# Starting two steps of the next attention block ahead of the last token tile's transposes

## The chip, the cores and the metric

The kernel runs on all 8 cores of one Trainium2 chip. Each core computes one batch element of the input, on its own, with no exchange between cores. The metric is the device time of one execution in microseconds (us), that of the slowest core.

Engines are named as the profile names them: PE is TensorE (PEld its weight loads), DVE is VectorE, ACT is ScalarE, POOL is GpSimd, SP is SyncE. A "q" behind an engine's name is its sequencer.

## The reference

```python
x = L0_attn_x                                  # 8 x 4096 x 1024, float32
q, k, v = x @ w_q, x @ w_k, x @ w_v            # one head of 128
A = softmax(q @ k.T / sqrt(128))               # 4096 x 4096 for each batch element
x = layernorm(x + ((A @ v) * mask) @ w_o)
# feed-forward with ternary weights and activations rounded to 8 bits a row
gate = silu(act_quant(x) @ quant(w_gate).T)    # 1024 -> 4096
up   = act_quant(x) @ quant(w_up).T
x = layernorm(x + act_quant(gate * up) @ quant(w_down).T)
```

`quant(w)` needs the mean of |w| over the whole matrix, then turns each weight into -1, 0 or 1 times a scale. `act_quant` needs the largest |x| of each row.

## The kernel before

The program is written engine by engine: each of three phases has one block per engine, and the order within a block is the order of the code. Engines meet only at semaphores (`sm[...]`), which count up.

**Phase AB** (`_phase_AB`) is the one that is changed. First q, k and v are projected (`qt`, `kt`, `vt`), and v is transposed to `vtok`. Then the attention runs over 8 blocks `qb` (0 to 7) of 512 queries. A block has a *loop* and a *tail*.

- The loop runs over 32 steps `kc` of 128 keys. In a step PE multiplies the scores into `ps_s` (L566), ACT takes the exponential of them into `pbuf` (L478), and PE adds `pbuf` times v into `ps_h` (L570) and the row sums into `ps_r` (L572). `ps_s` and `pbuf` have two buffers each, and PE's waits let the scores of step kc+1 be computed only behind the products of step kc (L566 to L574).
- The tail takes 4 tiles of 128 tokens (`sc` = 4·qb to 4·qb+3). When the loop's last sum is there (`avrs`), DVE copies the sums to `rsb` and takes their reciprocal. For each tile PE multiplies by w_o into `ps_y1` (L598, L600), DVE adds the residual, makes the layer norm (with a square root on ACT in its middle, L496), and rounds the row to `xqdq` (L438, semaphore `xqd`). PE then transposes `xqdq` into `ps_tr` with 8 small products (`_xtr`, L590, semaphore `xtr`), and ACT copies `ps_tr` to `xqs` (`_xtre`, L490, semaphore `xtre`). `ps_tr` has one buffer, so each set of transposes waits for the copy of the one before.

The copies lag. ACT copies the tiles 4·qb and 4·qb+1 in the tail, and the last two tiles at the head of the next block (L471 to L473, `_xtre_head`). PE transposes the tile 4·qb+2 in the tail, behind the products of the last tile, and the last tile 4·qb+3 at the head of the next block (L552 to L559), ahead of everything else there.

DVE has a second job in this phase, the weights. Ahead of the loops' end in blocks 0, 1 and 2 it sums |w| over 32 chunks of 128 x 1024 each (`w1_chunks`, L349), which SP loads from HBM into the two buffers `wstf`. From block 4 on it turns the chunks into ternary weights, 6 behind each tile (`w2_chunks`, L442), and POOL stores them. Between blocks 2, 3 and 4 PE has a tiny product at the block's head (L543, L548), which makes the weight scales.

**Phase C1** computes gate and up (L783, L789) with the ternary weights, and rounds and transposes the result. **Phase C2** multiplies by w_down (L946) and makes the second layer norm.

Of the kernel before, what the change touches and what calls it, by code (L numbers as in the profile page):

```python
# [22 lines left out]
NHC = D // P  # L23
# [110 lines left out]
def _phase_AB(nc, sm, d, pers):  # L134
    ones_b = pers["ones_b"]; onesf = pers["onesf"]; ones1f = pers["ones1f"]
    identb = pers["identb"]; identf = pers["identf"]
# [7 lines left out]
             (d["wuT"], d["wuqs"], NHC, 4, 1024, 1),  # L144
             (d["wdT"], d["wdqs"], NOC, 1, 1024, 2)]
    n_wch = sum(r * c for _, _, r, c, _, _ in wplan)
    wsched = []
    for c in range(4):
# [13 lines left out]
    def SB(name, shape, dt):  # L162
        return es.enter_context(nc.sbuf_tensor(name, shape, dt))
    def PS(name, shape, dt):
        return es.enter_context(nc.psum_tensor(name, shape, dt))
    with es:
# [20 lines left out]
        xqdq = SB("xqdq", [P, 2, D], BF16)  # L187
# [6 lines left out]
        ps_tr = PS("ps_tr", [P, 1024], BF16)  # L194
# [250 lines left out]
        @blk.scalar  # L445
        def _(s):
            s = _AD(s)
            def _xtre_head(s, sc):
                j = sc % 4
                s.wait_ge(sm["xtr"], sc + 1)  # L450
                if sc >= 4 and j == 0:
                    qbp = sc // 4 - 1
                    s.wait_ge(sm["xqsp0" if qbp % 2 == 0 else "xqsp1"],
                              16 * NHC * (qbp // 2 + 1))
                s.copy(xqs[:, :, j * 128:(j + 1) * 128],
                       ps_tr[:].rearrange("p (a b) -> p a b", a=8)
                       ).then_inc(sm["xtre"], 1)
            for sb in range(NQB):
                s.wait_ge(sm["qkv"], (sb + 1) * 3)
                s.copy(qt[:, sb * 512:(sb + 1) * 512], ps_s[:, 0, :])  # L460
                s.copy(kt[:, sb * 512:(sb + 1) * 512], ps_s[:, 1, :])
                s.copy(vt[:, sb * 512:(sb + 1) * 512], ps_h[:]
                       ).then_inc(sm["qkve"], 1)
            for gidx in range(8):
                s.wait_ge(sm["vtr"], gidx + 1)
                s.copy(vtok[:, gidx * 4:(gidx + 1) * 4, :],
                       ps_vt[:].rearrange("p (a b) -> p a b", a=4)
                       ).then_inc(sm["vtre"], 1)
            for qb in range(NQB):
                base = qb * 32  # L470
                if qb >= 1:  # L471
                    for scp in (qb * 4 - 2, qb * 4 - 1):
                        _xtre_head(s, scp)  # L473
                for kc in range(32):
                    s.wait_ge(sm["ss"], base + kc + 1)
                    if kc >= 2:
                        s.wait_ge(sm["avrs"], base + kc - 1)
                    s.activation(pbuf[:, kc % 2, :], ps_s[:, kc % 2, :],  # L478
                                 ACTF.Exp, bias=0.0, scale=ATT_SCALE
                                 ).then_inc(sm["pexp"], 1)  # L480
                s.wait_ge(sm["avrs"], (qb + 1) * 32)
                s.copy(htb[:], ps_h[:]).then_inc(sm["hev"], 1)
                def _xtre(s, sc):
                    j = sc % 4
                    s.wait_ge(sm["xtr"], sc + 1)
                    if sc >= 4 and j == 0:
                        qbp = sc // 4 - 1
                        s.wait_ge(sm["xqsp0" if qbp % 2 == 0 else "xqsp1"],
                                  16 * NHC * (qbp // 2 + 1))
                    s.copy(xqs[:, :, j * 128:(j + 1) * 128],  # L490
                           ps_tr[:].rearrange("p (a b) -> p a b", a=8)
                           ).then_inc(sm["xtre"], 1)
                for j in range(4):
                    sc = qb * 4 + j
                    s.wait_ge(sm["z1"], 2 * (sc + 1))
                    s.activation(stats[:, 5:6], stats[:, 4:5], ACTF.Sqrt,  # L496
                                 bias=0.0, scale=1.0).then_inc(sm["sqrt1"], 1)
                    if j >= 2:
                        _xtre(s, sc - 2)
                if qb == NQB - 1:  # L500
                    _xtre(s, qb * 4 + 2)
                    _xtre(s, qb * 4 + 3)

        @blk.tensor
        def _(t):
# [32 lines left out]
            for qb in range(NQB):  # L538
                base = qb * 32
                qsl = slice(qb * 512, (qb + 1) * 512)  # L540
                if qb == 3:
                    t.wait_ge(sm["wabs"], n_wch + 1)
                    t.matmul(pv32[0:1, 0:4], onesf[:], wacc[:],  # L543
                             start=True, stop=True)
                    t.drain().then_inc(sm["wsum"], 1)
                if qb == 4:
                    t.wait_ge(sm["wscal"], 1)
                    t.matmul(pv32[:, 4:12], ones1f[:], srow[:],  # L548
                             start=True, stop=True)
                    t.drain().then_inc(sm["wbc"], 1)  # L550
                if qb >= 1:
                    sc3 = qb * 4 - 1  # L552
                    t.wait_ge(sm["xqd"], sc3 + 1)
                    t.wait_ge(sm["xtre"], sc3)
                    for ic in range(NHC):
                        t.transpose(ps_tr[:, ic * 128:(ic + 1) * 128],
                                    xqdq[:, sc3 % 2, ic * 128:(ic + 1) * 128],
                                    identb[:])
                    t.drain().then_inc(sm["xtr"], 1)  # L559
                    t.wait_ge(sm["hev"], qb)  # L560
                    t.wait_ge(sm["rdone"], qb)
                    t.wait_ge(sm["pexp"], base)
                for kc in range(32):
                    if kc >= 2:
                        t.wait_ge(sm["pexp"], base + kc - 1)
                    t.matmul(ps_s[:, kc % 2, :], kt[:, kc * 128:(kc + 1) * 128],  # L566
                             qt[:, qsl], start=True, stop=True
                             ).then_inc(sm["ss"], 1)
                    t.wait_ge(sm["pexp"], base + kc + 1)
                    t.matmul(ps_h[:], vtok[:, kc, :], pbuf[:, kc % 2, :],  # L570
                             start=(kc == 0), stop=(kc == 31))
                    t.matmul(ps_r[:], ones_r[:], pbuf[:, kc % 2, :],  # L572
                             start=(kc == 0), stop=(kc == 31)
                             ).then_inc(sm["avrs"], 1)  # L574
                t.wait_ge(sm["rdone"], qb + 1)
                if qb >= 1:
                    t.wait_ge(sm["z1"], 8 * qb)
                for j in range(4):
                    t.transpose(ps_y1[:, 0, j:j + 1],
                                rinv[0:1, j * 128:(j + 1) * 128],  # L580
                                identf[0:1, 0:1])
                t.drain().then_inc(sm["rcolT"], 1)
                t.wait_ge(sm["hev"], qb + 1)
                t.wait_ge(sm["rcole"], qb + 1)
                def _xtr(t, sc):
                    t.wait_ge(sm["xqd"], sc + 1)
                    if sc >= 1:
                        t.wait_ge(sm["xtre"], sc)
                    for ic in range(NHC):
                        t.transpose(ps_tr[:, ic * 128:(ic + 1) * 128],  # L590
                                    xqdq[:, sc % 2, ic * 128:(ic + 1) * 128],
                                    identb[:])
                    t.drain().then_inc(sm["xtr"], 1)
                for j in range(4):
                    sc = qb * 4 + j
                    if sc >= 1:
                        t.wait_ge(sm["z1"], 2 * sc)
                    t.matmul(ps_y1[:, 0, :], htb[:, j * 128:(j + 1) * 128],  # L598
                             wob[:, 0:512], start=True, stop=True)
                    t.matmul(ps_y1[:, 1, :], htb[:, j * 128:(j + 1) * 128],  # L600
                             wob[:, 512:1024], start=True, stop=True
                             ).then_inc(sm["y1"], 1)
                    if j >= 1:
                        _xtr(t, qb * 4 + j - 1)
                if qb == NQB - 1:
                    _xtr(t, qb * 4 + 3)
# [371 lines left out]
```

## Time and profile before

| | us |
|---|---|
| median of 2 runs | 4078.61 (4067.52 and 4089.70) |
| the profiled execution, its own time | 4072.59 |
| its span on the slowest core (core 5) | 4070.8 |
| spans of the 8 cores | 4046.7 to 4070.8 |
| granted TensorE clock, mean of each core | 0.695 to 0.697 |
| busy on core 5: PE / DVE / ACT | 2086.7 / 2291.9 / 535.4 |

All positions below are microseconds from the start of the span of core 5. The attention's loops and tails run from 160 to about 1745, C1 from there to about 3500, C2 to the end. A row of the timeline gives the start, the duration, the engine, the line, the operation with output and input, and in brackets how long the engine had been idle before it and what ended that. L53 and L54 are the lines of a helper, which issues most instructions of DVE, ACT and POOL; there the names of the tiles tell which one it is. `ps_y` in a row is `ps_y1` here.

### The profile page before, as it was taken

The numbers are of one execution on the slowest core, as the hardware profiler recorded it, in microseconds if no ns is written. First come the engines' busy times: TensorE is split into PE (matmuls) and PEld (weight loads), VectorE is DVE, ScalarE is ACT, GpSimd is POOL, SyncE is SP. The second block draws the span as 40 slices with busy tenths as digits, with TensorE's granted clock in tenths as the row PEclk, the third lists the DMA queues.
The fourth block names the chain that finished last, engine by engine and source line by source line (L and its number), as shares of the span: only waits on it lengthen the run. The fifth ranks groups of instructions, "written<-read, shape, count | busy, mean of one in ns | idle before, by whom it ended". The sixth has DMA issues, their size and how long they took to land. (4 is left out here: it accounts for less than half of the span.)

```text
span 4070.8 us, 32582 instructions; the slowest of 8 cores (4046.7 to 4070.8 us)
## 1 busy us (share of the span) xinstructions
PE 2086.7 (51%) x8516; PEld 937.5 (23%) x8516; DVE 2291.9 (56%) x3888; ACT 535.4 (13%) x794; POOL 244.0 (6%) x359
## 2 busy tenths in 40 slices
PE   4535244250413214047483929384756657179998
PEld 2312111120101101012231313132322223124443
DVE  2145653517365463736757575857576666535555
ACT  0212111120201111001211111111111111100000
POOL 1000000001101010100000000000000000000000
PEclk8655555555555555579695959697877879589999
DMA  8405241105344251444242424333333332364441
GB/s 238 134 31 175 93 134 42 36 26 140 97 114 124 67 147 60 134 140 135 63 143 54 146 62 128 87 116 94 104 104 93 114 83 83 84 209 138 159 135 62
DMA packets 290771, 440.43 MB, mean 108 GB/s; under 512 B 12960, under 2 KB 220832, under 8 KB 290592
## 3 DMA queue, kind: packets, MB, share of 16 engines
q1 hardware_dynamic: 240784, 285.77, 24.4%
q0 software_dynamic: 49808, 152.59, 12.4%
q8 instruction: 74, 1.21, 0.1%
q14 instruction: 105, 0.86, 0.1%
HBM read 337.64 MB, written 100.66 MB: 108 GB/s over the span
## 5 line engine op out<-in xcount | busy, mean ns | idle before, releaser
L783 PE MATMUL ps_g<-wgu,xqr 128*128 128x512 bf16 x2048 | 496.4, 386 | 151.8 <-issue 92.4
L946 PE MATMUL ps_y<-wdq,hqr 128*128 128x512 bf16 x2048 | 453.9, 382 | 69.5 <-DMA wdq<-wdqs 59.1
L789 PE MATMUL ps_u<-wgu,xqr 128*128 128x512 bf16 x2048 | 485.2, 380 | 0.0
L803 PE MATMUL ps_t<-identb,hq 128*128 128x128 bf16 x1024 | 129.5, 307 | 581.8 <-DVEq L743 455.6
L53 DVE TENSOR_SCALAR gtr<-ps_g,scv 128x512 f32<-128x512 f32 x256 | 192.1, 750 | 250.1 <-PEq L794 249.9
L570 PE MATMUL ps_h<-pbuf,vtok 128*128 128x512 f32 x256 | 195.9, 765 | 244.6 <-ACTq L54 244.6
L53 DVE TENSOR_TENSOR hp<-sgt,ps_u 128x512 f32<-128x512 f32 x256 | 175.8, 687 | 241.8 <-ACTq L54 241.8
L590 PE MATMUL ps_tr<-identb,xqdq 128*128 128x128 bf16 x200 | 25.3, 307 | 526.2 <-ACTq L54 435.1
L783 PEld LDWEIGHTS ps_g<-wgu,xqr 128*128 128x128 bf16 x2048 | 184.4, 98 | 458.8 <-issue 282.3
L53 ACT ACTIVATE sgt<-gtr 128x512 f32<-128x512 f32 x256 | 161.1, 629 | 874.0 <-DVEq L54 874.0
L946 PEld LDWEIGHTS ps_y<-wdq,hqr 128*128 128x128 bf16 x2048 | 199.2, 98 | 323.9 <-issue 93.5
L789 PEld LDWEIGHTS ps_u<-wgu,xqr 128*128 128x128 bf16 x2048 | 201.3, 98 | 245.1 <-issue 6.3
L803 PEld LDWEIGHTS ps_t<-identb,hq 128*128 128x128 bf16 x1024 | 99.1, 138 | 614.0 <-issue 614.0
L53 DVE COPY rsb<-ps_r 1x512 f32<-1x512 f32 x8 | 5.4, 679 | 417.2 <-PE ps_r L572 416.8
L53 ACT ACTIVATE pbuf<-ps_s 128x512 fp32r<-128x512 f32 x256 | 152.9, 597 | 482.6 <-PE ps_s L566 482.5
L53 DVE TENSOR_REDUCE stats<-wstf 128x1 f32<-128x1024 f32 x96 | 117.1, 1220 | 172.6 <-DMA wstf<-wgT 66.8
L53 ACT COPY hqts<-ps_t 128x1024 bf16<-128x1024 bf16 x128 | 129.6, 1012 | 576.7 <-PEq L807 576.7
L53 DVE TENSOR_SCALAR wc<-wstf,whm 128x1024 f32<-128x1024 f32 x192 | 144.7, 754 | 80.8 <-DMA wstf<-wgT 25.5
L53 DVE TENSOR_REDUCE stats<-hp 128x1 f32<-128x512 f32 x256 | 175.6, 686 | 21.5 <-issue 1.3
L53 DVE SCALAR_TENSOR_TENSOR z2t<-ps_y,yscale,x1r 128x512 f32<-128x512 f32 x64 | 48.0, 751 | 223.7 <-PEq L951 221.3
L570 PEld LDWEIGHTS ps_h<-pbuf,vtok 128*128 128x128 f32 x256 | 73.5, 287 | 419.9 <-issue 419.9
L677 POOL DMA_DIRECT2D hqTs<-hqts x32 | 63.6, 1987 | 1715.2 <-ACTq L54 1715.2
(104 smaller groups left out, 2371.9 us busy)
## 6 DMA issues: line engine op xcount, KB each, us to landing
wgu<-wgqs SPq DMA_DIRECT2D x64, 1024.0 KB, 7.5
wgu<-wuqs SPq DMA_DIRECT2D x64, 1024.0 KB, 9.8
wstf<-wgT SPq DMA_DIRECT2D x64, 512.0 KB, 4.9
wstf<-wuT SPq DMA_DIRECT2D x64, 512.0 KB, 4.8
wstf<-wdT SPq DMA_DIRECT2D x64, 512.0 KB, 3.9
hqTs<-hqts POOLq DMA_DIRECT2D x32, 1024.0 KB, 8.5
hqr<-hqTs SPq DMA_DIRECT2D x32, 1024.0 KB, 9.9
xts<-xT POOLq DMA_DIRECT2D x8, 2048.0 KB, 14.3
```

Of the source, the lines that this page charges most:

```text
L53: f(*a, **k)
L570: t.matmul(ps_h[:], vtok[:, kc, :], pbuf[:, kc % 2, :], start=(kc == 0), stop=(kc == 31))
L590: t.transpose(ps_tr[:, ic * 128:(ic + 1) * 128], xqdq[:, sc % 2, ic * 128:(ic + 1) * 128], identb[:])
L677: gp.dma_start(out=d["hqTs"].rearrange("(a p) s -> p a s", p=P)[:, :, gsc * 128:(gsc + 1) * 128], in_=hqts[:, gsc % 2, :, :]).then_inc(sm[ ...
L783: t.matmul(ps_g[:, sc % 2, :], xqr[:, sb % 2, ic, sc * 128:(sc + 1) * 128], wgu[:, idx % 2, 0, ic, :], start=(ic == 0), stop=(ic == NHC - 1))
L789: t.matmul(ps_u[:, sc % 2, :], xqr[:, sb % 2, ic, sc * 128:(sc + 1) * 128], wgu[:, idx % 2, 1, ic, :], start=(ic == 0), stop=(ic == NHC - 1))
L803: t.transpose(ps_t2[:, k * 128:(k + 1) * 128], hq[:, gsc % 2, oc * 128:(oc + 1) * 128], identb[:])
L946: t.matmul(ps_y2[:, sc % 3, hf, :], hqr[:, pr % 4, oc, (sc % 2) * DH:(sc % 2 + 1) * DH], wdq[:, oc, hf * 512:(hf + 1) * 512], start=(oc == ...
```

## The change

Three pieces of code move; nothing is computed otherwise. On ACT the two copies at a block's head (tiles 4·qb-2 and 4·qb-1) move behind the exponential of the block's step 1. On PE the transposes of tile 4·qb-1 move from ahead of the block's step 0 into its step 1, between the scores and the wait for the exponential. The waits of the block's head for `hev`, `rdone` and `pexp` stay ahead of step 0.

```diff
@@ ACT
             for qb in range(NQB):
                 base = qb * 32
-                if qb >= 1:
-                    for scp in (qb * 4 - 2, qb * 4 - 1):
-                        _xtre_head(s, scp)
                 for kc in range(32):
                     s.wait_ge(sm["ss"], base + kc + 1)
                     if kc >= 2:
...
                                  ACTF.Exp, bias=0.0, scale=ATT_SCALE
                                  ).then_inc(sm["pexp"], 1)
+                    if qb >= 1 and kc == 1:
+                        _xtre_head(s, qb * 4 - 2)
+                        _xtre_head(s, qb * 4 - 1)
@@ PE
                 if qb >= 1:
-                    sc3 = qb * 4 - 1
-                    t.wait_ge(sm["xqd"], sc3 + 1)
-                    t.wait_ge(sm["xtre"], sc3)
-                    for ic in range(NHC):
-                        t.transpose(ps_tr[:, ic * 128:(ic + 1) * 128],
-                                    xqdq[:, sc3 % 2, ic * 128:(ic + 1) * 128],
-                                    identb[:])
-                    t.drain().then_inc(sm["xtr"], 1)
                     t.wait_ge(sm["hev"], qb)
                     t.wait_ge(sm["rdone"], qb)
                     t.wait_ge(sm["pexp"], base)
...
                     t.matmul(ps_s[:, kc % 2, :], kt[:, kc * 128:(kc + 1) * 128],
                              qt[:, qsl], start=True, stop=True
                              ).then_inc(sm["ss"], 1)
+                    if qb >= 1 and kc == 1:
+                        sc3 = qb * 4 - 1
+                        t.wait_ge(sm["xqd"], sc3 + 1)
+                        t.wait_ge(sm["xtre"], sc3)
+                        for ic in range(NHC):
+                            t.transpose(ps_tr[:, ic * 128:(ic + 1) * 128],
+                                        xqdq[:, sc3 % 2,
+                                             ic * 128:(ic + 1) * 128],
+                                        identb[:])
+                        t.drain().then_inc(sm["xtr"], 1)
                     t.wait_ge(sm["pexp"], base + kc + 1)
                     t.matmul(ps_h[:], vtok[:, kc, :], pbuf[:, kc % 2, :],
```

PE, from the end of block 0's tail into block 1, in the kernel before:

```order
L598 MATMUL ps_y<-wob,htb 128x512
L600 MATMUL ps_y<-wob,htb 128x512
L590 MATMUL ps_tr<-identb,xqdq 128x128 x8
L556 MATMUL ps_tr<-identb,xqdq 128x128 x8
L566 MATMUL ps_s<-qt,kt 128x512
L570 MATMUL ps_h<-pbuf,vtok 128x512
L572 MATMUL ps_r<-pbuf,ones_r 1x512
L566 MATMUL ps_s<-qt,kt 128x512
L570 MATMUL ps_h<-pbuf,vtok 128x512
```

The same place in the changed kernel, whose lines have other numbers (its L558 is L566 before, its L566 is L556 before, its L572 and L574 are L570 and L572):

```order
L600 MATMUL ps_y<-wob,htb 128x512
L602 MATMUL ps_y<-wob,htb 128x512
L592 MATMUL ps_tr<-identb,xqdq 128x128 x8
L558 MATMUL ps_s<-qt,kt 128x512
L572 MATMUL ps_h<-pbuf,vtok 128x512
L574 MATMUL ps_r<-pbuf,ones_r 1x512
L558 MATMUL ps_s<-qt,kt 128x512
L566 MATMUL ps_tr<-identb,xqdq 128x128 x8
L572 MATMUL ps_h<-pbuf,vtok 128x512
L574 MATMUL ps_r<-pbuf,ones_r 1x512
```

The 8 transposes of the last tile moved behind 4 products of the next block: the scores, the product with v and the sums of step 0, and the scores of step 1. This holds in blocks 1 to 7.

ACT at the same place, the changed kernel against the one before (`stats` is the square root, `xqs` the copies, `pbuf` the exponentials):

```order
 L53 COPY xqs<-ps_tr 128x8x128
 L53 ACTIVATE stats<-stats 128x1
-L53 COPY xqs<-ps_tr 128x8x128 x3
-L53 ACTIVATE pbuf<-ps_s 128x512 x32
+L53 COPY xqs<-ps_tr 128x8x128
+L53 ACTIVATE pbuf<-ps_s 128x512 x2
+L53 COPY xqs<-ps_tr 128x8x128 x2
+L53 ACTIVATE pbuf<-ps_s 128x512 x30
```

Of the three copies in a row the first stays behind the last square root of the tail, and the other two moved behind the second exponential.

## Rows read from the trace of the kernel before

**Rows 1.** Windows: a tail, a loop, most of phase C1; busy us by engine, PE clock.
```profile
242.00:319.00 77.00, 9.37 (x44) 5.60 (x44) 60.92 (x120) 5.53 (x9) 3.71 (x7) 0.50 0.14 48
...
654.00:737.00 83.00, 51.95 (x96) 19.69 (x96) 0.20 (x1) 21.12 (x35) 4.81 (x9) 0.50 0.06 19
...
1745.00:2900.00 1155.00, 690.46 (x3291) 312.00 (x3292) 742.84 (x1178) 186.09 (x246) 41.14 (x23) 0.79 0.37 103
```

**Rows 2.** Who waited for whom, 150 to 1745: us in total, times, longest.
```profile
DVE rsb L53 <- PE ps_r L572: 416.8, 6, 88.0
...
PE ps_tr L556 <- DVEq L54: 54.6, 7, 8.2
```

**Rows 3.** Timeline of the first head, between block 0's tail and block 1's loop.
```profile
308.70 1.01 PE L590 MATMUL ps_tr<-identb,xqdq 128*128 128x128 bf16 x8 [14.50 <-ACTq L54]
...
316.39 1.22 DVE L53 SCALAR_TENSOR_TENSOR xqdq<-tiq,c1q 128x1024 bf16<-128x1024 int32 x1
...
317.89 1.01 PE L556 MATMUL ps_tr<-identb,xqdq 128*128 128x128 bf16 x8 [8.18 <-DVEq L54]
319.02 1.01 ACT L53 COPY xqs<-ps_tr 128x1024 bf16<-128x1024 bf16 x1 [8.18 <-PEq L559]
...
319.35 0.77 PE L566 MATMUL ps_s<-qt,kt 128*128 128x512 f32 x1 [0.44 <-issue]
...
320.19 1.28 ACT L53 ACT_TABLE_LOAD   x1 [0.16 <-PE ps_s L566]
...
321.49 0.60 ACT L53 ACTIVATE pbuf<-ps_s 128x512 fp32r<-128x512 f32 x1
...
322.25 0.77 PE L570 MATMUL ps_h<-pbuf,vtok 128*128 128x512 f32 x1 [2.14 <-ACTq L54]
...
323.97 0.60 ACT L53 ACTIVATE pbuf<-ps_s 128x512 fp32r<-128x512 f32 x1 [1.88 <-PE ps_s L566]
...
324.73 0.77 PE L570 MATMUL ps_h<-pbuf,vtok 128*128 128x512 f32 x1 [0.86 <-ACTq L54]
```

**Rows 4.** Timeline of PE and DVE: the ends of the loops of blocks 1, 2, 3.
```profile
401.59 0.63 PE L572 MATMUL ps_r<-pbuf,ones_r 128*1 128x512 f32 x1
...
409.81 0.68 DVE L53 COPY rsb<-ps_r 1x512 f32<-1x512 f32 x1 [0.19 <-issue]
...
570.11 0.63 PE L572 MATMUL ps_r<-pbuf,ones_r 128*1 128x512 f32 x1
...
575.76 0.68 DVE L53 COPY rsb<-ps_r 1x512 f32<-1x512 f32 x1 [0.23 <-issue]
...
736.79 0.68 DVE L53 COPY rsb<-ps_r 1x512 f32<-1x512 f32 x1 [83.67 <-PE ps_r L572]
```

**Rows 5.** Timeline of PE: the heads of blocks 3, 4 and 6.
```profile
652.38 1.01 PE L556 MATMUL ps_tr<-identb,xqdq 128*128 128x128 bf16 x8 [7.41 <-DVEq L54]
...
806.07 0.56 PE L548 MATMUL ps_vt<-srow,ones1f 1*128 1x8 f32 x2 [0.23 <-issue]
...
813.66 1.01 PE L556 MATMUL ps_tr<-identb,xqdq 128*128 128x128 bf16 x8 [7.04 <-DVEq L54]
...
1274.19 1.01 PE L556 MATMUL ps_tr<-identb,xqdq 128*128 128x128 bf16 x8 [7.83 <-DVEq L54]
```

**Rows 6.** Groups of DVE by line, 150 to 1745: count, busy us, mean ns.
```profile
L53 DVE TENSOR_REDUCE stats<-wstf 128x1 f32<-128x1024 f32 x66 | 80.5, 1220 | 90.2 <-DMA wstf<-wdT 41.4 <-DMA wstf<-wuT 25.3 <-DMA wstf<-wgT 22.4
...
L53 DVE TENSOR_REDUCE stats<-z1t 128x1 f32<-128x1024 f32 x32 | 39.0, 1220 | 3.8
```

**Rows 7.** Timeline of PE at the start of phase C1.
```profile
1782.02 3.57 PE L783 MATMUL ps_g<-wgu,xqr 128*128 128x512 bf16 x8 [54.01 <-DMA wgu<-wuqs]
...
1785.38 2.83 PE L789 MATMUL ps_u<-wgu,xqr 128*128 128x512 bf16 x8
...
1793.11 1.89 PE L783 MATMUL ps_g<-wgu,xqr 128*128 128x512 bf16 x8 [1.19 <-DVEq L54]
...
1794.83 1.89 PE L789 MATMUL ps_u<-wgu,xqr 128*128 128x512 bf16 x8
```

## The prediction

> **What bounds the kernel now.** I read the windows first, to see which engine each stretch hangs on. A tail (242 to 319) has DVE busy for 60.92 of its 77 us and PE for 9.37; a loop (654 to 737) has PE busy for 51.95 of 83 and DVE for 0.20 [rows 1]. So loops and tails stand one behind the other, each on its own chain, and what one leaves unused of the other's engine is lost. Then the waits: DVE waits for a loop's last sum 6 times in 8, 416.8 us in all, and PE waits for the rounded last tile at all 7 heads, 54.6 us in all, 7.8 each [rows 2]. That second wait is what the change goes at.
>
> The timeline of the first head shows it from inside [rows 3]. PE is free at 308.70 + 1.01 = 309.71, with the transposes of tile 2 done. DVE still rounds tile 3, until 316.39 + 1.22 = 317.61. PE's transposes of tile 3 start at 317.89, and only behind them come the scores of step 0 (319.35), a table load on ACT (320.19, 1.28), the exponential (321.49) and the product with v (322.25). The product of step 1 starts at 324.73. The loop's steps 0 and 1 need nothing of tile 3.
>
> Last the loops' ends, which tell in which blocks an earlier PE is worth anything [rows 4]. In block 3 the copy to `rsb` was released by PE, after 83.67 us of idle DVE. In blocks 1 and 2 it was not: PE's last sum ended at 402.22 and 570.74, and DVE came at 409.81 and 575.76, straight from its own weight chunks (idle 0.19 and 0.23). There DVE is late by 7.6 and 5.0 us. The 6 waits of rows 2 are blocks 0 and 3 to 7.
>
> **The change part by part.** No instruction is added or removed; the order moves at 7 heads.
>
> *PE, the new head.* Set on the clock of rows 3: the scores of step 0 start 0.44 behind PE's last instruction, as they do now, at 310.15. The first product with v comes 2.90 later (322.25 - 319.35, with the table load in it), at 313.05; it, the sums and the scores of step 1 follow. The second exponential starts 1.72 behind that product (323.97 - 322.25) and takes 0.60: 315.37. Then ACT copies tile 2: 0.16 to start, as behind `ps_s`, and 1.01, to 316.54, and PE knows it 0.28 later (317.61 to 317.89 is the same step from DVE). So the chain that the change puts ahead of the transposes is 0.44 + 2.90 + 1.72 + 0.60 + 0.16 + 1.01 + 0.28 = 7.11 us long, and it lies in a gap of 8.18. The transposes still start at 317.89, on the wait for DVE. Behind them the product of step 1 starts as the scores of step 0 did, 1.46 later (319.35 - 317.89), its exponential long there: at 319.35 instead of 324.73. **A head gains 5.38 us.**
>
> *ACT.* The copy of tile 3 stands ahead of the exponential of step 2. It ends at 319.02 + 1.01 = 320.03, as now; the exponential of step 2 can't start before 319.35 + 1.72 = 321.07. So the copy delays nothing, and `xqs` is complete, and stored by POOL, at the time it is now.
>
> *How thin the cover is.* The gap that must hold the 7.11 us is 7.41 in block 3, 7.04 in block 4 (behind the small product of L548, which ends at 806.63), 7.83 in block 6 [rows 5]; of 54.6 us in 7, none of the others is under 7.8. Block 4 loses 0.07; the rest lose nothing.
>
> *What the table load costs.* The row has 1.28 us, and the exponential starts 0.02 behind it [rows 3]. That is the price I use, and it now lies beside DVE's work. The Trainium skill (page ScalarE: Activation LUTs, section What ACT_TABLE_LOAD costs) counts a drain of about 1.38 us on top, 2.66 for a switch. This case's trace shows no such drain between the load and the exponential. By the page the chain would be over 8.4 us and longer than every gap, and the gain smaller by up to 4.4 us.
>
> *Copies between exponentials.* They could ask for further table loads. In the rows now a copy stands ahead of the load and `Exp` behind it; no row has an `xqs` copy under `Exp`. I take nothing; the bound above is one load (1.28) in front of the copies and one in front of step 2, below.
>
> *Which heads count.* Heads 3 to 7 pass on what they gain: 5 x 5.38 - 0.07 = 26.8 us. In blocks 1 and 2 PE gains 5.38 too and then waits longer for DVE, whose chunks come no earlier (they start behind tile 3 and wait for SP's loads). **0 there.** Below: 0 at all heads, if a wait that I don't see takes over; above: all 7, 37.7 us, if the chunks happened to come faster.
>
> *What runs beside.* For 7 us a head PE and ACT now work next to DVE's layer norm. A DVE reduction of 128 x 1024 takes 1220 ns in the tail (of `z1t`, PE nearly idle) and 1220 ns over the weight chunks, most of which run beside a loop [rows 6]. So I charge nothing. The clock can't fall: it is at 0.50 (1.2 GHz) in loop and tail alike [rows 1].
>
> *The sum.* The profiled execution took 4072.6 us; less 26.8 that is 4045.8. It lies 6.0 below the median of the two runs (4078.6), from which the sum gives 4051.8. I take the middle, **4049**. C1 and C2 come earlier by 27 us and are otherwise the same.
>
> **The rivals.**
>
> *A. All seven heads count.* DVE's slack in blocks 1 and 2 would have to be gone. Against it stand idle times of 0.19 and 0.23 on DVE there. Gain 37.7: 4038.
>
> *B. Nothing is gained.* The wait for tile 3 only moves by two steps, and something later in the block takes the 5 us back. For it: the wait is still there. Against it: each step of a loop waits only for the step before. 4076.
>
> *C. More table work on ACT.* A copy that changes the table would put 1.28 ahead of tile 2's copy: the chain is 8.39, past the gaps of blocks 3 and 4 by 0.98 and 1.35, of the three others by up to 0.56 each. With another load ahead of step 2 (ready at 321.3, not 321.1) it is some 5 us in all: 4054. The page's rule above, with its 1.38, would end at the same 4053 to 4054.
>
> *D. Slower: phase C1 meets a lower clock.* C1 starts 27 us earlier against whatever sets its clock, which averages 0.79 there [rows 1]. At 1.2 GHz 8 gate products start within 3.36 us (1782.02 to 1785.38), at 2.4 GHz within 1.72 (1793.11 to 1794.83) [rows 7]; a group of 16 costs 3.3 us more at the lower level. If over 8 more of C1's 256 groups fall there, and PE is what those wait for, the gain is gone; with 12 more it is 4049 + 40 = 4089. For it: the two runs before lie 22 us apart. Against it: nothing in C1 depends on when it starts.
>
> **How the numbers follow.** The forecast has 0.80, A 0.05, B 0.05, C 0.06, D 0.04. All of them but a far end of A or D lie within 2% (82 us) of before, which is about what a measurement can tell from no change: faster by more 0.01, within 0.98, slower by more 0.01. The scatter of the runs is 11 us to either side of their median. The range takes that around 4049, with A and C inside: 4034 to 4070; it leaves out B and D.
>
> **What would show it right or wrong.** In the profile after: at each head PE's scores of step 0 directly behind the transposes of tile 2; the transposes of tile 3 released by DVE and not by ACT, after some 3 us of idle and not 8; the product of step 1 some 1.5 us behind their start. PE's wait for the rounded tile shrinks from 7.8 to about 3 a head. The `rsb` copies of blocks 1 and 2 stay where they are, and from block 3 on each comes 5.4 us earlier than the last, C1's first product 27 us earlier than 1782. The count of table loads stays. Wrong would be: `rsb` of block 1 or 2 released by DVE later than now, the tile-3 transposes released by ACT, or C1 at another clock.

## The result and the profile after

The changed kernel takes 4041.4 us (median of 12 runs, 4032.7 to 4061.1) against 4067.5 for the kernel before (11 runs). The ratio is 0.9934, 95% interval 0.9917 to 0.9952: 27 us less, between 20 and 34. In some executions the cores of one die are granted a lower clock and take longer; the ratios leave these executions out. The profiled execution took 4037.0 us; its slowest core is core 6, with a span of 4035.1.

The timeline of the first head in the kernel after answers to [rows 3]. Its lines are two higher than before; L558 is the scores, L566 the transposes of tile 3, L572 the product with v.

```profile
307.41 1.01 PE L592 MATMUL ps_tr<-identb,xqdq 128*128 128x128 bf16 x8 [14.50 <-ACTq L54]
...
308.86 0.77 PE L558 MATMUL ps_s<-qt,kt 128*128 128x512 f32 x1 [0.44 <-issue]
309.71 1.28 ACT L53 ACT_TABLE_LOAD   x1 [2.47 <-PE ps_s L558]
311.00 0.60 ACT L53 ACTIVATE pbuf<-ps_s 128x512 fp32r<-128x512 f32 x1
...
311.76 0.77 PE L572 MATMUL ps_h<-pbuf,vtok 128*128 128x512 f32 x1 [2.14 <-ACTq L54]
...
313.48 0.60 ACT L53 ACTIVATE pbuf<-ps_s 128x512 fp32r<-128x512 f32 x1 [1.88 <-PE ps_s L558]
314.23 1.01 ACT L53 COPY xqs<-ps_tr 128x1024 bf16<-128x1024 bf16 x1 [0.15 <-issue]
...
316.63 1.01 PE L566 MATMUL ps_tr<-identb,xqdq 128*128 128x128 bf16 x8 [3.25 <-DVEq L54]
317.75 1.01 ACT L53 COPY xqs<-ps_tr 128x1024 bf16<-128x1024 bf16 x1 [2.51 <-PEq L570]
317.87 0.76 PE L572 MATMUL ps_h<-pbuf,vtok 128*128 128x512 f32 x1 [0.23 <-issue]
```

The scores of step 0 start 0.44 behind the transposes of tile 2, the table load now runs while DVE still works on tile 3, and the transposes of tile 3 are still released by DVE, after 3.25 us of idle and not 8.18. The product of step 1 starts 1.24 behind their start; before it was 324.73 - 317.89 = 6.84. This head gains 5.60 us.

The ends of the loops of blocks 1 to 4 on DVE, and the heads of blocks 4 and 6, in the timeline of the kernel after:

```profile
411.46 0.68 DVE L53 COPY rsb<-ps_r 1x512 f32<-1x512 f32 x1 [0.18 <-issue]
...
574.16 0.68 DVE L53 COPY rsb<-ps_r 1x512 f32<-1x512 f32 x1 [0.23 <-issue]
...
729.67 0.68 DVE L53 COPY rsb<-ps_r 1x512 f32<-1x512 f32 x1 [78.06 <-PE ps_r L574]
...
799.99 0.77 PE L558 MATMUL ps_s<-qt,kt 128*128 128x512 f32 x1 [0.44 <-issue]
...
805.07 1.22 DVE L53 SCALAR_TENSOR_TENSOR xqdq<-tiq,c1q 128x1024 bf16<-128x1024 int32 x1
805.36 1.01 ACT L53 COPY xqs<-ps_tr 128x1024 bf16<-128x1024 bf16 x1 [0.15 <-issue]
...
806.58 1.01 PE L566 MATMUL ps_tr<-identb,xqdq 128*128 128x128 bf16 x8 [2.07 <-ACTq L54]
...
885.40 0.68 DVE L53 COPY rsb<-ps_r 1x512 f32<-1x512 f32 x1 [78.20 <-PE ps_r L574]
...
1252.29 1.01 PE L566 MATMUL ps_tr<-identb,xqdq 128*128 128x128 bf16 x8 [2.87 <-DVEq L54]
```

Blocks 1 and 2 still end on DVE, with 0.18 and 0.23 of idle [rows 4]; block 3's wait is 78.06 in place of 83.67. In block 4, the one with no cover to spare, ACT's copy ends at 806.37 and DVE's rounding at 806.29, and the transposes are released by ACT. The distance between the `rsb` copies of blocks 2 and 4 holds two heads, two loops and two tails without weight chunks, and so is free of what DMA adds elsewhere: 898.08 - 575.76 = 322.3 us before, 885.40 - 574.16 = 311.2 after, 5.5 a head. Below it is "distance 2 to 4".

The profile has the same copies on the other cores. Over the 8 cores of each profiled execution, the mean distance from block 2's to block 7's copy, which holds the five heads 3 to 7, fell from 1007.0 to 978.7 us: 28.3, or 5.7 a head. The mean distance from block 0's to block 2's, which holds heads 1 and 2, was 335.9 before (330.0 to 340.8 on single cores) and 334.8 after (333.1 to 337.5): no gain that stands out of that spread. And a tail is as long as before: from block 1's copy to the transposes of its last tile, next to which PE and ACT now work, it is 76.62 us before (409.81 to 486.43) and 76.63 after (411.46 to 488.09).

Who waited for whom, 150 to 1755, kernel after:

```profile
DVE rsb L53 <- PE ps_r L574: 390.0, 6, 91.4
...
PE ps_tr L566 <- DVEq L54: 17.8, 6, 3.2
```

PE's wait for the rounded tile fell from 54.6 us in 7 [rows 2] to 17.8 in 6, and the seventh is a wait of 2.1 for ACT. Windows of 1750 us of phase C1, before (1755 to 3505) and after (1720 to 3470):

```profile
1755.00:3505.00 1750.00, 1061.94 (x5064) 479.37 (x5064) 1140.90 (x1809) 284.46 (x378) 60.14 (x31) 0.80 0.35 100
```

```profile
1720.00:3470.00 1750.00, 1054.01 (x4976) 479.55 (x5064) 1141.95 (x1810) 284.79 (x378) 60.50 (x31) 0.80 0.33 100
```

The mean clock is 0.80 in both; C1 only starts earlier (1782.02 before, 1746.35 after). These 35.7 us are more than the measured 27, as they compare two single executions on different cores.

### The profile page after: what moved, and what is told of

It reads as the page before. It is cut to its first block and busy times, and to the rows that moved or that the text cites. A ratio compares the mean times of both kernels' runs of the same rounds, so it can differ in the third digit from the quotient of the medians.

```text
span 4035.1 us, 32453 instructions; the slowest of 8 cores (4013.1 to 4035.1 us)
## 1 busy us (share of the span) xinstructions
PE 2075.0 (51%) x8387; PEld 936.5 (23%) x8516; DVE 2293.0 (57%) x3888; ACT 535.4 (13%) x794; POOL 245.0 (6%) x359
## 5 line engine op out<-in xcount | busy, mean ns | idle before, releaser
L572 PE MATMUL ps_h<-pbuf,vtok 128*128 128x512 f32 x256 | 195.9, 765 | 240.4 <-ACTq L54 238.6
L592 PE MATMUL ps_tr<-identb,xqdq 128*128 128x128 bf16 x200 | 25.3, 306 | 524.1 <-ACTq L54 432.9
L572 PEld LDWEIGHTS ps_h<-pbuf,vtok 128*128 128x128 f32 x256 | 73.5, 287 | 412.5 <-issue 412.5
```

The costliest lines, as they stand in the source:

```text
L572: t.matmul(ps_h[:], vtok[:, kc, :], pbuf[:, kc % 2, :], start=(kc == 0), stop=(kc == 31))
L592: t.transpose(ps_tr[:, ic * 128:(ic + 1) * 128], xqdq[:, sc % 2, ic * 128:(ic + 1) * 128], identb[:])
```

## The experiments

Ratios are to the kernel before in the same series, whose median was 4062 to 4065 us; the microseconds beside them are the ratio times that. Single positions are those of the slowest core. Which heads count comes first, then how far the steps can be moved, then what bounds the loop.

**Only heads 1 and 2, only heads 3 to 7**

```diff
-                    if qb >= 1 and kc == 1:
+                    if 1 <= qb <= 2 and kc == 1:
```

with the code of before at the other heads; the second kernel has `qb >= 3` there.

> The new order at heads 1 and 2 alone; heads 3 to 7 as before. Theory (those heads are absorbed by DVE's weight chunks): PE's last sum of blocks 1 and 2 ends 5 to 6 us earlier against the head, DVE copies to rsb when it did before, with under 0.3 us of idle, and the time stays within the scatter, about 0 us of gain. Rival (every head counts alike): 2 x 5.6 = 11 us less than before, and rsb released by PE.

Ratio 1.000 (0.998 to 1.002). The timeline of this kernel, PE's last sum of block 2 and DVE behind it:

```profile
578.27 0.63 PE L586 MATMUL ps_r<-pbuf,ones_r 128*1 128x512 f32 x1
...
587.36 0.68 DVE L53 COPY rsb<-ps_r 1x512 f32<-1x512 f32 x1 [0.23 <-issue]
```

PE ends 587.36 - 578.90 = 8.5 us ahead of DVE, where it was 5.0 before, and DVE takes no notice. How much of the 3.5 is the head can't be read, since the chunks themselves come a few us earlier or later in each execution. But DVE's copies come no sooner: block 0's to block 2's is 336.8 us on the mean of the 8 cores, against 335.9 before. The rival's 11 us lie outside the interval, which reaches to 8 us of gain.

> The new order at heads 3 to 7 alone. Theory: 5 x 5.6 = 28 us less than before, as much as the whole change. Rival (every head counts alike): 5/7 of the change's 26 us, 19 us.

Ratio 0.9937 (0.9924 to 0.9951): 26 us (20 to 31), the whole change; the rival's 19 lie just outside. Distance 2 to 4 is 311.1.

**The first pass's chunks split 48, 24, 24**

```diff
-                    w1_chunks(32)
+                    w1_chunks((48, 24, 24)[qb])
```

> The kernel before, with the 96 weight chunks of the first pass split 48, 24, 24 over blocks 0, 1, 2 in place of 32, 32, 32. Theory (DVE ends the loops of blocks 1 and 2, 7.6 and 5.0 us behind PE): rsb of blocks 1 and 2 is released by PE, 12.6 us less than before. Rival (PE sets these ends too): 0.

> The changed kernel with the same 48, 24, 24. Theory: now all 7 heads count, so it lies 7 x 5.6 = 39 us below the kernel before with that split, 52 us below the kernel before. Rival (heads 1 and 2 give nothing for another reason than DVE's chunks): 28 us below that kernel, 41 below the kernel before.

The ratios are 0.9971 (0.9953 to 0.9989), 12 us, and 0.9868 (0.9849 to 0.9886), 54 us (46 to 61); the rivals' 0 and 41 lie outside. The `rsb` copies of blocks 1 and 2 in the timeline, the order of before first, the changed one second:

```profile
398.37 0.68 DVE L53 COPY rsb<-ps_r 1x512 f32<-1x512 f32 x1 [15.27 <-PE ps_r L572]
...
559.42 0.68 DVE L53 COPY rsb<-ps_r 1x512 f32<-1x512 f32 x1 [19.91 <-PE ps_r L572]
```

```profile
401.54 0.68 DVE L53 COPY rsb<-ps_r 1x512 f32<-1x512 f32 x1 [9.88 <-PE ps_r L574]
...
557.16 0.68 DVE L53 COPY rsb<-ps_r 1x512 f32<-1x512 f32 x1 [14.89 <-PE ps_r L574]
```

Now PE releases both. From one to the other it is 161.05 us with the old order (165.95 in [rows 4]), and 155.62 with the new: 4.9 us were DVE's lateness, and a further 5.4 are the head, which was worth nothing as long as DVE came last. Block 1 shows the same. From block 0's copy to its own it is 167.99 us in the kernel before (from 241.82 to 409.81), 160.56 with the other split (from 237.81) and 155.00 with the new order as well (from 246.54): 7.4 and 5.6.

**One step in place of two**

```diff
-                    if qb >= 1 and kc == 1:
+                    if qb >= 1 and kc == 0:
```

> The transposes and both copies move by one step (into step 0) in place of two. Theory: what counts is the work put ahead of DVE's rounded tile: the first product with v comes 1.24 us behind the start of the transposes in place of 4.36, 3.1 us a head (the table load among them), 16 us in all. Rival (the gain comes from the hidden table load and not from the steps): the same 28 us as with two steps. Rival (the load stays on the path): 1.8 us a head, 9 us.

Distance 2 to 4 is 899.63 - 583.61 = 316.0, that is 3.15 a head, as expected. In the first head:

```profile
316.01 1.01 PE L566 MATMUL ps_tr<-identb,xqdq 128*128 128x128 bf16 x8 [6.97 <-DVEq L54]
317.25 0.76 PE L572 MATMUL ps_h<-pbuf,vtok 128*128 128x512 f32 x1 [0.23 <-issue]
```

The ratio, 0.9983 (0.9963 to 1.0003), is 7 us, between 15 and nothing, where 16 were expected. The heads show no loss: from block 2's to block 7's copy it is 990.0 us on the mean of the 8 cores, 17.0 less than before, so the five heads give what was expected. A part of the shortfall stands ahead of them: block 0's to block 2's copy, where DVE's chunks decide, took 339.7 us (333.2 to 345.3 on single cores) against 335.9 before. Whether the order of this kernel delays these chunks or the execution had them late isn't shown, and the rest is open.

**Two steps, but the copy of tile 2 left at the head**

```diff
+                if qb >= 1:
+                    _xtre_head(s, qb * 4 - 2)
                 for kc in range(32):
...
-                        _xtre_head(s, qb * 4 - 2)
```

> As the change, but ACT's copy of tile 2 stays at the head, ahead of the exponential of step 0. Theory (the cover hides ACT's chain whole, but for 0.07 us in block 4): the same time as the change, 28 us below before, and the transposes of all 7 heads released by DVE, block 4's too. Rival (the copy's place matters, as it delays the first exponential or the table load): 1 us a head, 5 us slower than the change. The distance of the rsb copies of blocks 2 and 4: 311.2 by the theory, over 312 by the rival.

Ratio 0.9937 (0.9913 to 0.9961), distance 311.2. In the waits all 7 transposes are released by DVE:

```profile
PE ps_tr L567 <- DVEq L54: 19.9, 7, 3.2
```

So ACT's two copies are hidden whole. The time alone couldn't tell (16 to 35 us less than before, which holds the rival's 23); the distance does.

**Three steps**

```diff
-                    if qb >= 1 and kc == 1:
+                    if qb >= 1 and kc == 2:
```

> As the change, but both copies and the transposes one step later still, in step 2. Theory (the cover is 8.18 us and the chain ahead of the transposes, 7.11 us in the change, is now 2.53 longer, 9.64): the transposes are released by ACT and no more by DVE, PE stands still for the copy of tile 2, and a head gains 6.7 us against before, 1.1 more than the change and not 2.5 more; some 33 us in all. Rival (the wait for DVE's rounded tile still decides): 8.1 us a head, 40 us. Judged by the distance of the rsb copies of blocks 2 and 4, which holds two heads and no weight chunks: 322.3 us before, 311.2 with the change; 309.0 by the theory, 306.2 by the rival.

Ratio 0.9922 (0.9904 to 0.9939), 32 us. The waits turn over:

```profile
PE ps_tr L566 <- ACTq L54: 14.6, 7, 2.1
```

Distance 2 to 4 is 310.8, not 309.0. The theory was right and its sum careless: it took the gap of the first head, 8.18, for heads 3 and 4, whose gaps are 7.41 and 7.04 [rows 5], 0.77 and 1.14 less. With those the gain is 5.9 and 5.6 in place of 6.7, and 322.3 - 11.5 = 310.8. Past the cover PE stands still for ACT's copy. The time alone doesn't part this kernel from the change (25 to 39 us against 20 to 34), but the rival's 40 lie just outside.

**Step 4, with the copy of tile 2 still in step 1**

```diff
                     if qb >= 1 and kc == 1:
                         _xtre_head(s, qb * 4 - 2)
+                    if qb >= 1 and kc == 4:
                         _xtre_head(s, qb * 4 - 1)
...
-                    if qb >= 1 and kc == 1:
+                    if qb >= 1 and kc == 4:
                         sc3 = qb * 4 - 1
```

> The copy of tile 2 behind the exponential of step 1 as in the change, but the transposes of tile 3 in step 4 and its copy behind the exponential of step 4. Theory (the loop may start whenever PE is free, and the transposes then fit into PE's idle time of a step): the first product with v comes 9.2 us earlier than before, the transposes cost 0.3 us behind the 0.92 us that PE idles in a step: 8.9 us a head, 44 us in all. Rival (transposes and copy in a running loop cost their full 2.4 us): 6.8 us a head, 34 us. Rival (the wait for tile 3 was all there was to gain, and the change has it): no more than the change, 28 us.

Ratio 0.9895 (0.9880 to 0.9910): 43 us (37 to 49), 16 more than the change, outside both rivals. The head as it stands in PE's timeline:

```profile
316.53 0.77 PE L573 MATMUL ps_h<-pbuf,vtok 128*128 128x512 f32 x1 [0.92 <-ACTq L54]
...
317.52 0.63 PE L559 MATMUL ps_s<-qt,kt 128*128 128x512 f32 x1
317.95 1.08 PE L567 MATMUL ps_tr<-identb,xqdq 128*128 128x128 bf16 x8
...
319.26 0.77 PE L573 MATMUL ps_h<-pbuf,vtok 128*128 128x512 f32 x1 [0.23 <-issue]
```

The transposes wait for nobody. The product comes 319.26 - 316.53 = 2.73 us behind the one of step 3, against 2.53 in an ordinary step: they cost 0.20. Distance 2 to 4 is 304.8 on the slowest core and 305.7 on the mean of the 8.

**The orders side by side**

Means over the 8 cores of each profiled execution, in us between `rsb` copies. The last column is the gain of the five heads 3 to 7 against before, and behind it the gain that was expected for them, as far as a sum was on record.

| order | block 0 to 2 | 2 to 4 | 2 to 7 | gain of five heads |
|---|---|---|---|---|
| before | 335.9 | 322.4 | 1007.0 | |
| new at heads 1 and 2 | 336.8 | 322.4 | 1005.9 | 1.1 (0) |
| one step | 339.7 | 316.1 | 990.0 | 17.0 (16) |
| two steps, the change | 334.8 | 311.2 | 978.7 | 28.3 (26.8) |
| two steps at heads 3 to 7 | 337.3 | 311.2 | 977.3 | 29.6 (28) |
| two steps, a copy left | 334.5 | 311.2 | 977.0 | 30.0 (28) |
| three steps | 335.9 | 310.7 | 973.3 | 33.7 (33) |
| tile 3 in step 4 | 336.5 | 305.7 | 962.8 | 44.2 (44) |

Kernels with the same five heads differ by up to 1.7 us in the last column, which is its scatter. No order gains in blocks 1 and 2 beyond the spread of the single cores. In the other five the gain goes as the theory of the cover has it, step by step.

**Scores one step ahead of the exponential**

```diff
+                _score(0)
                 for kc in range(32):
-                    if kc >= 2:
-                        t.wait_ge(sm["pexp"], base + kc - 1)
-                    t.matmul(ps_s[:, kc % 2, :], kt[:, kc * 128:(kc + 1) * 128],
-                             qt[:, qsl], start=True, stop=True
-                             ).then_inc(sm["ss"], 1)
+                    if kc + 1 < 32:
+                        _score(kc + 1)
...
                     t.wait_ge(sm["pexp"], base + kc + 1)
```

`_score(kc)` is the wait and the product that were taken out.

> The changed kernel, with PE's scores of step kc+1 issued ahead of the wait for the exponential of step kc. Theory (a step of 2.53 us is a round trip between PE and ACT, and PE idles 0.92 of it): a step falls to PE's own work, start to start 0.43 + 0.56 + 0.43 or some 1.5 us, 30 us a block in blocks 0 and 3 to 7, 180 us in all below the changed kernel; blocks 1 and 2 end with DVE's chunks as before. Rival (PE's products take their recorded 2.0 us of each step): 0.5 us a step, about 95 us in all. Rival (the scores ahead only shift the wait): 0.

Ratio 0.9257 (0.9224 to 0.9291), where the changed kernel has 0.9934: 275 us below it, not 180. Windows of this kernel on its slowest core: the end of block 0's loop, the head of block 3, the rest of its loop, and the rest of block 4's.

```profile
160.00:186.00 26.00, 25.16 (x84) 10.45 (x83) 0.00 (x0) 16.63 (x28) 0.00 (x0) 1.00 0.00 1
595.00:607.00 12.00, 8.38 (x23) 4.39 (x24) 4.68 (x9) 5.54 (x8) 4.27 (x8) 0.50 0.25 90
608.00:631.00 23.00, 21.45 (x75) 9.29 (x74) 0.00 (x0) 14.96 (x26) 0.54 (x1) 1.00 0.07 24
...
718.00:741.00 23.00, 22.81 (x72) 10.06 (x71) 0.00 (x0) 13.74 (x23) 0.54 (x1) 0.82 0.07 23
```

In the loops PE is busy almost without a break, and its clock goes from 0.50 (1.2 GHz) to 1.00 (2.4 GHz). In block 4 the mean is only 0.82; why, no run shows. The scores in block 3's loop:

```profile
602.03 0.63 PE L558 MATMUL ps_s<-qt,kt 128*128 128x512 f32 x1
...
606.67 0.63 PE L558 MATMUL ps_s<-qt,kt 128*128 128x512 f32 x1
...
607.64 0.40 PE L558 MATMUL ps_s<-qt,kt 128*128 128x512 f32 x1
...
608.77 0.40 PE L558 MATMUL ps_s<-qt,kt 128*128 128x512 f32 x1
...
611.42 0.40 PE L558 MATMUL ps_s<-qt,kt 128*128 128x512 f32 x1
```

At first, with the clock still at 0.50, three steps take 4.64 us, 1.55 a step: that is the 1.5 that was expected. Then four steps take 3.78 us, 0.95 a step, where the same loop took 2.53. The forecast had the order right and no faster clock in it. Block 3 takes 108.8 us between `rsb` copies (523.17 to 632.01) in place of 155.5, block 4 110.7 in place of 155.7. Between the profiled executions of the two kernels block 0 ends 53.8 us earlier (186.66 and not 240.50) and blocks 3 to 7 take 236.6 less (743.8 and not 980.4). Blocks 1 and 2 take 2.9 more, as DVE ends them, and the rest of the program 17 more, which leaves 271 of the 290.

**All three together**

> Scores ahead, transposes of tile 3 in step 4 and the 48, 24, 24 split together. Theory: scores ahead as in its own run, 16 us more from step 4, and 8 chunks less of 2.87 us in blocks 1 and 2 each, 46 us, as DVE ends both there: some 60 us below the kernel with scores ahead alone. Rival (block 0's loop, now 30 us shorter, is ended by its 48 chunks): about 20 to 30 us less of that.

Ratio 0.9133 (0.9117 to 0.9149), a median of 3713.0 us: by the ratios 50 us below the last one. The `rsb` copies of blocks 0, 2 and 7 in its timeline:

```profile
201.59 0.68 DVE L53 COPY rsb<-ps_r 1x512 f32<-1x512 f32 x1 [0.19 <-issue]
...
488.69 0.68 DVE L53 COPY rsb<-ps_r 1x512 f32<-1x512 f32 x1 [0.23 <-issue]
...
1225.07 0.68 DVE L53 COPY rsb<-ps_r 1x512 f32<-1x512 f32 x1 [0.18 <-issue]
```

DVE ends six of eight blocks: 0 to 2 and 5 to 7. That is why 50 us came and not 60. Against the last kernel, on the slowest core of each, blocks 1 and 2 are 49.4 us shorter, as expected (46); block 0, with its 48 chunks, is 14.9 longer (201.59 in place of 186.66), which was the rival's condition; and step 4 pays in blocks 3 and 4 alone, 7.3 us, while blocks 5 to 7, now ended by DVE, take 524.1 in place of 524.3. This is the fastest version found, 8.7% below the kernel before.

**And 8 chunks of the second pass at the head of block 4**

```diff
@@ DVE, behind whm
+                    w2_chunks(8)
@@ POOL, ahead of the wait for x1q
+                if sc == 16:
+                    wsp_chunks(8)
```

> The version with scores ahead, step 4 and the 48, 24, 24 split, and 8 chunks of the second weight pass moved from the last tiles to the head of block 4's loop (their stores too), where DVE idles 28.7 us. Theory (DVE is the bound of blocks 5 to 7 there, and a chunk costs it some 3.2 us): block 4 gets no longer by more than 2 us, and 8 x 3.2 = 26 us less in the last tiles, about 3687 us. Rival (weight loads or stores by DMA decide, not DVE's place): under 10 us.

Ratio 0.9143 (0.9103 to 0.9184), no difference from the version without that could be told. The 26 us of the forecast lie outside the interval; but the ratio rests on two executions, 3700.6 and 3732.5, so a gain of some 10 us or a loss of some 20 stays possible. DVE's timeline in block 4, with POOL's in the middle:

```profile
687.57 1.58 DVE L53 TENSOR_SCALAR wc<-wstf,whm 128x1024 f32<-128x1024 f32 x2 [2.19 <-DMA wstf<-wgT]
...
688.47 0.80 POOL L249 DMA_DIRECT2D xo<-x  x1 [5.11 <-DMA xqTs<-xqs]
689.26 1.07 POOL L261 DMA_DIRECT2D wgqs<-wqzb  x2
...
695.53 1.23 DVE L53 TENSOR_TENSOR wqzb<-wc 128x1024 bf16<-128x1024 f32 x1 [6.38 <-DMA wgqs<-wqzb]
...
719.44 0.68 DVE L53 COPY rsb<-ps_r 1x512 f32<-1x512 f32 x1 [0.19 <-issue]
```

The third chunk waited 6.38 us for the store of the first, which POOL issued at 689.26, only behind its wait for the `xqTs` stores (5.11). Distance 2 to 4 grew from 212.2 to 227.1: the 8 chunks took 15 us more than DVE's idle time had room for. The last tail got it back: from block 7's copy to C1's first product it is 165.1 us (1245.99 to 1411.04) against 193.1 in the version without (1225.07 to 1418.18), 28 less. So C1 starts 7 us earlier there; the measured times are too few to show it.

## Why the prediction was right

- **The wait and its place.** Right. PE's wait for tile 3 was 7.8 us a head, and steps 0 and 1 fit in front of it; moving one, two or three steps gives 17.0, 28.3 and 33.7 us in five heads.
- **5.38 us a head.** 5.60 in the first head, 5.5 by the distance 2 to 4, 5.7 over five heads and 8 cores. The difference is the issue time behind the transposes, 0.23 and not 0.44 (the product of step 1 starts 1.24 behind their start, and not 1.46). 5 x 5.6 = 28 us against a measured 27. The gain is under 2%, as forecast.
- **The chain of 7.11 us in the gap.** Right to the thinnest place: block 4, forecast 0.07 short, is the only head that ACT releases. The chain itself is 7.03 there (799.55 to 806.58): PE starts 0.21 behind ACT's copy, and not the 0.28 that was taken from DVE. So the head loses nothing: PE idles 2.07 there, and 2.08 with a copy left at the head, where DVE releases it. A step more (9.64 by the sum) put ACT last at every head.
- **Nothing at heads 1 and 2.** Shown from both sides: alone they give 0, and once DVE has fewer chunks there they give 5.6 and 5.4.
- **7.6 and 5.0 us of DVE lateness.** Shown by the split of the chunks: 7.4 and 4.9 by the `rsb` copies, 12 us by the ratio.
- **The table load.** 1.28 us, and the exponential 0.01 behind its end in the head after. The drain of some 1.38 us that the Trainium skill (page ScalarE: Activation LUTs, section What ACT_TABLE_LOAD costs) adds to it isn't in this trace either: by it ACT would have released the transposes at every head, and it did so at one. ACT's instructions by line in the kernel after have 18 loads, as the kernel before has, so copies between exponentials ask for none:

```profile
L53 ACT ACT_TABLE_LOAD  x18: 1283/1283/1283, 42.0 to 3582.0; - x18
```

- **What runs beside.** Charged at nothing, and rightly: the tail of block 1 is 76.62 us before and 76.63 after.
- **The signs.** Two of the three that were to show it wrong appeared. ACT released the transposes of block 4, which the prediction itself expected by its 0.07. And block 1's `rsb` copy came at 411.46, 1.65 later than before; but the chunks place it anywhere from 398 to 414 on the 8 cores of the executions before and after, so this sign could tell nothing. C1's first product came 35.7 us earlier and not 27, of which some 8 are scatter between two executions.
- **The rivals.** A (all heads) needs the other chunk split and is then true. B (nothing gained) falls by the distance 2 to 4, C (more table work) by that and by the count of 18 loads. D (C1 at a lower clock) falls by the windows, 0.80 in both.
- **The level.** The forecast, 4049, was worked from a profiled execution and a median of two runs; with 11 runs the kernel before lies at 4067.5 and not at 4075.6, and the forecast of 26.8 us less from there is 4040.7, against 4041.4. The size was right and the level 8 us off; that the range held the result owes something to its width of 36 us.

What the prediction missed is what it didn't ask. It took the loop's 2.53 us a step as given, though [rows 1] have PE busy for 52 of a loop's 83 us and at half clock; the time to be had there was ten times what the change found.

## What to carry to other kernels

When work is moved ahead of a wait, add up the chain that now runs in front of it, and hold it against the wait's length at every place where it occurs: the gain grows by a full step as long as the chain fits, and by what is left over after that. Then ask at each place who is last: a gain on an engine that another one outlasts anyway is worth nothing until that one is relieved, and the two changes are then worth more together (54 us) than each alone (27 and 12). And where two engines hand a tile back and forth in every step of a loop, issue the next step's product ahead of the wait first: here that gave 275 us, and the head of the loop 27.

## What was unexpected of the hardware

With 0.92 us of idle in every 2.53 us step PE was granted 0.50 of its clock in the loops, before and after the change and on all 8 cores. With the idle gone, the slowest core was granted 0.50 at the head and in the first steps of a loop, and then 1.00, except in block 4, where the rest of the loop had 0.82. Products of 128 x 512 went from 0.63 to 0.40 us as the profile records them. Removing the idle so paid twice: about 1 us a step was expected and came at the lower clock, and at the higher one it was 1.6. The Trainium skill (page TensorE: Matmul & The Clock Gate, section Part 1: The HAM clock gate) says that the lower clock is the default and that activity releases it, which agrees with these windows. What the runs add is a loop of 80 us in which PE works in every step and its clock stays down all the same.
